# First x asked for after VectorE's first memset, and 16 warm-up matmuls

## The reference

```python
y = x[b] @ weight[adapter_ids[b]].T              # 256 x 1024
logits = y @ gate_w.T + expert_bias              # 4 experts
one_hot = one_hot(argmax(logits))
z = einsum('nh,erh->ner', y, lora_A)             # 4 experts x rank 8
delta = einsum('ner,ehr->neh', z, lora_B) picked by one_hot
out = x[b] + y @ W_up.T + delta
```

## Time and profile before

| what | us |
|---|---|
| median of three runs | 374.62 |
| the profiled execution | 374.81 |
| its span, first to last instruction | 373.0 |
| TensorE busy in it | 367.5 |
| VectorE, ScalarE busy | 262.4, 159.4 |
| first real matmul | 8.45 after the span's start |

### The profile page before, as it was taken

One profiled execution on the slowest core, in us unless ns is written; L12 is line 12 of the kernel. 1 busy time (PEld: TensorE's weight loads), 2 busy tenths in 40 slices (PEclk: granted clock), 3 DMA queues, 4 the chain that ended last, 5 costly groups with the idle time before them and its releaser, 6 DMA issues.

```text
span 373.0 us, 6260 instructions
## 1 busy us (share of the span) xinstructions
PE 367.5 (99%) x2348; PEld 334.7 (90%) x2348; DVE 262.4 (70%) x519; ACT 159.4 (43%) x320; POOL 6.6 (2%) x18
## 2 busy tenths in 40 slices
PE   7999999999999999999999999999999999999996
PEld 5888888888888999889998899989999899988996
DVE  4777587696758988678755786567874777746752
ACT  5667363642527543465115651155513553144300
POOL 1000500000000000000000000000000000000000
PEclk9999999999999999999999999999999999999999
DMA  7999975871069730687026760376404861160002
GB/s 244 402 394 312 408 286 182 325 226 57 0 192 340 252 119 0 226 302 243 21 96 210 270 216 3 147 250 231 163 2 178 324 213 76 49 234 0 2 1 114
DMA packets 19598, 68.19 MB, mean 183 GB/s; under 512 B 2288, under 2 KB 2416, under 8 KB 19568
## 3 DMA queue, kind: packets, MB, share of 16 engines
q1 hardware_dynamic: 19280, 66.74, 50.0%
q10 hardware_dynamic: 288, 1.05, 0.8%
HBM read 59.39 MB, written 8.39 MB: 182 GB/s over the span
## 4 chain that ended last, share of the span: by engine, by line
PE 97%; SPq 1%; DMA 1%; DVE 0%; issue 0%; ACT 0%; DVEq 0%
PE ps_y L785 31%; PE ps_u L796 19%; PE ps_y L787 16%; PE ps_v L796 10%; PE ps_p L796 5%; PE ps_u L803 2%; PE ps_v L803 2%; PE ps_u L807 2%; PE ps_v L805 2%; PE ps_u L805 2%; PE ps_v L807 2%; PE ps_p L816 1%; DMA w_raw<-w_dram 1%; SPq L241 1%; PE ps_p L847 0%; PE ps_v L847 0%
## 5 line engine op out<-in xcount | busy, mean ns | idle before, releaser
L785 PE MATMUL ps_y<-x_hilo,w_hi 128*128 128x512 f32 x512 | 178.3, 392 | 0.3 <-DVE w_lo L510 0.3
L787 PE MATMUL ps_y<-x_hilo,w_lo 128*128 128x256 f32 x512 | 143.2, 280 | 0.0
L785 PEld LDWEIGHTS ps_y<-x_hilo,w_hi 128*128 128x128 f32 x512 | 95.8, 187 | 22.1 <-DVE w_lo L510 0.8
L787 PEld LDWEIGHTS ps_y<-x_hilo,w_lo 128*128 128x128 f32 x512 | 96.7, 189 | 0.1
L517 DVE TENSOR_TENSOR w_lo<-w_raw,w_hi 128x512 fp32r<-128x512 f32 x126 | 81.3, 688 | 16.9 <-ACT w_hi L376 16.2
L376 ACT CAST w_hi<-w_raw 128x512 fp32r<-128x512 f32 x126 | 71.8, 624 | 3.4 <-DMA w_raw<-w_dram 3.3
L391 ACT COPY small<-ps_y 128x256 f32<-128x256 f32 x64 | 23.8, 372 | 107.2 <-PE ps_y L787 107.0
L562 DVE TENSOR_TENSOR y_raw<-ps_y,small 128x256 f32<-128x256 f32 x64 | 27.2, 425 | 47.1 <-ACT small L391 47.1
L796 PE MATMUL ps_u<-up_lo,y_parts 128*128 128x256 f32 x192 | 38.4, 281 | 0.0
L796 PE MATMUL ps_u<-wide_hi,y_parts 128*128 128x256 f32 x192 | 34.8, 293 | 0.0
L573 DVE TENSOR_TENSOR y_parts<-y_raw,y_parts 128x512 fp32r<-128x512 f32 x50 | 32.5, 687 | 1.3 <-ACT y_parts L394 0.9
(11 more groups left out here) (108 smaller groups left out, 393.7 us busy)
## 6 DMA issues: line engine op xcount, KB each, us to landing
w_raw<-w_dram SPq DMA_DIRECT2D x64, 512.0 KB, 4.4
rows<-x_dram SPq DMA_DIRECT2D x16, 512.0 KB, 5.7
out_dram<-rows SPq DMA_DIRECT2D x15, 512.0 KB, 2.6
x_raw<-xT_dram SPq DMA_DIRECT2D x14, 512.0 KB, 5.0
up_raw<-w_up_dram SPq DMA_DIRECT2D x8, 512.0 KB, 12.4
wide_stage<-w_up_dram SPq DMA_DIRECT2D x4, 512.0 KB, 14.0
thin_stage<-w_up_dram SPq DMA_DIRECT2D x4, 512.0 KB, 9.4
x_raw<-xT_dram ACTq DMA_DIRECT2D x2, 512.0 KB, 4.2
```

Source lines behind the costliest of these rows:

```text
L785: pe.matmul(ps_y[c % 2][:, :], w_hi[:, n % RING, cols], x_hilo[:, :, k, :], start=(k == 0), stop=False)
L787: last = pe.matmul(ps_y[c % 2][:, S:2 * S], w_lo[:, n % RAWS, cols], x_hilo[:, 0, k, :], start=False, stop=(k == KC - 1))
```

## The change

ScalarE waits, ahead of its two requests for the first x, for `warm_step` to be 1, that is for the end of VectorE's first memset. Nothing else in ScalarE's order moves. The number of matmuls on zeros goes from 18 to 16.

```diff
-    WARM = 18
+    WARM = 16
...
+            act.wait_ge(warm_step, 1)
             for d in range(XD):
                 ks = slice(d * XS, (d + 1) * XS)
                 act.dma_start(x_raw[:, 1, ks, :], xT[0, :, ks, :]).then_inc(x_raw_in[d], 16)
```

## The result

The changed kernel takes 375.67 us, the median of 15 runs (375.01 to 375.89); the kernel before takes 375.08 in 15 runs (374.54 to 375.44). The ratio is 1.0014, with a 95% interval of 1.0008 to 1.0021: slower by 0.5 us, clear of noise, and inside the 0.2% that was set as the bound of "same". The profiled execution took 375.59, with a span of 373.8, against 374.81 and 373.0 before.

A forecast was written before the change was run, and what follows sets the result against it. TensorE bounds the kernel, leaving only the start: x's second half landing late puts the first real matmul at 9.32, plus 5.69 makes 15.01 against 14.38, so +0.6 us on 374.62, median 375.2; range 374.1 to 375.8.

The forecast's parts named there:

- What bounds the kernel: Whole kernel: TensorE is busy throughout the middle, so only the start and the wait ahead of block 2 can move the end.
- the hole ahead of block 2: Batch 0, between blocks 1 and 2: TensorE waits 0.24 us for VectorE's y_full, behind slice 2; absorbs part of a shift.
- (1) The wait: ScalarE at the start: x asked for 0.71 us later, at about 1.45; the table load behind it costs nothing.
- (3) The index load: SyncE's second register load at the start: falls from 1.99 to 1.49 us, so w is asked for at 3.75, not 4.25.
- rival B: SyncE's start: index load falls to 0.46, w asked for at 2.72, first real matmul 9.65, +0.96, 375.6; chance 0.18.
- (4) The sharing: DMA engines at the start: x and w share, x's second half lands last at 7.50, first real matmul at 9.32.
- the halves: DMA engines at the start: x and w each get half of 414 GB/s; x through at 7.05, w's slice about 7.1.
- x undisturbed: DMA engines at the start: one bound of the sharing, x not slowed by w, its second half there at 6.46.
- the 1.82 behind x's half: Start: 1.82 us of casts and subtractions from the landing of x's second half to the first real matmul.
- (5) The warm-up: TensorE's start: two zeros matmuls fewer end the warm-up at 7.65 instead of 8.11, which gains nothing.
- The sum: Whole kernel: first real matmul at 9.32 plus 5.69 gives 15.01 instead of 14.38; about +0.6 us, median 375.2.
- Rival A: SyncE's start: index load stays 1.99, x's second half lands 6.88, first real matmul 8.70, 374.9; chance 0.18.

The follow-up runs named there:

- Both late: Changed kernel with SyncE held by dummy memsets so w is asked for at 4.14, x still after the memset: 375.18 against 374.90 before, ratio 1.0008.
- 16 matmuls alone: Kernel before with 16 warm-up matmuls instead of 18, no wait of ScalarE: 374.79 against 374.93, ratio 1.0004.
- before, slices 1 to 3 held: Kernel before, SyncE asking for slice 1 of w only once x's second half landed, 14 warm-up matmuls: 375.28 against 374.90, ratio 1.0013.
- slice 0 and x alone: Changed kernel, SyncE waiting for both halves of x to land before asking for slice 1 of w: 375.69 against 374.93 before, ratio 1.0021.
- the wait alone: Changed kernel with 18 warm-up matmuls instead of 16: 375.56 against 374.93 for the kernel before, ratio 1.0017.
- with the 2 KB request: Changed kernel, ScalarE asking for the 2 KB bias ahead of its wait instead of SyncE: 375.70 against 374.93 for the kernel before, ratio 1.0022.
- half of x at the start: Changed kernel, only x's second half waiting for the memset, the first asked for at 0.74: 375.28 against 374.82 before, ratio 1.0017.
- x's second half behind: Changed kernel, x's second half on SyncE's queue behind slice 0, its third quarter taken later, 14 warm-up matmuls: 376.75 against 374.82 before, ratio 1.0055.
- the same, first half at the start: x's second half on SyncE's queue behind slice 0, but without ScalarE's wait, first half asked for at 0.74: 376.31 against 374.82 before, ratio 1.0037.

## Why the prediction held, and where it didn't

It gave 375.2 from a median of 374.62, +0.6; measured is +0.6 between the medians of 15 (375.67 - 375.08), 0.5 by the ratio. The sign, the size and the place are right. But several of its steps were off and made up for each other: that the number came out so near is in part luck.

- **What bounds the kernel: right.** Nothing moved but the start, the hole ahead of block 2, and the cadence of batch 0.
- **(1) The wait: right.** x's requests went out at 1.44, 0.70 later, and the table load ran from 2.33, hidden.
- **(3) The index load: mis-sized.** I took 1.49 from the sums of later pairs, which hide that the second load of a pair alone took 0.45 to 0.46 in four of them and 1.44 to 1.52 in two. Here it is 0.46 to 0.47, once 0.69, when x's transfer isn't under way. That is the end I had named as rival B. The 459 ns amid full traffic misled me into thinking that traffic doesn't matter; at the start it does, in all six profiles in which x is asked for at 0.74.
- **(4) The sharing: it costs, as I had it, but the share and the loser were wrong.** By the halves x's second half should have landed last, at 7.50 (and at 7.83 with the load at 0.46); it was cast at 6.98. Slice 0 was to be cast at 7.7 and was at 8.27. Nothing was shared evenly: x, asked for first, had the engines alone until 5.60, and of the 1.24 MB moved by 6.50 only 0.19 are w's. In bytes my bound "x undisturbed" was the nearer one, though x's last packets then came until 6.8 beside w's, and by 6.2 where w was asked for late. The Trainium skill's rule that I had set beside mine ("DMA: Bandwidth & Descriptors", Queues, rings and completion order) doesn't show as an even split here, since SyncE's queue got no turn between its request at 2.90 and 5.60. Whether its packets waited at the engines or hadn't been made yet, no view tells. From 5.60 on, slice 0 also shared with slices 1 to 3 (below). So the 1.82 behind x's half never counted: 0.92 behind slice 0 did. Rival B's price was too high for this reason: 9.65 against 9.19.
- **(5) The warm-up: right, nothing** (1.0004, 0.9993 to 1.0014), with one thing that I had considered only for the changed kernel: in executions where the clock rises late, the 18 matmuls hold up the kernel *before* (8.87, where slice 0 allowed 8.48).
- **The sum.** It was +0.87 at the first matmul by me and is +0.74 measured. The hole ahead of block 2 was given back as said, since slices 1 and 2 were there in good time (ScalarE's casts of them ran from 10.02 without a wait). Then +0.28 of cadence that no step had.
- **Rival A as an experiment.** Both late gives the first matmul at 8.70, the very figure of A. That is luck again: A had x's second half land last, at 6.88, and in the run slice 0 did (x's third cast began by 6.5). The difference from there to 9.19 is the price of asking for w early, slices 1 to 3 included: 0.49, and 0.6 by the second profile of the changed kernel (9.33). The measured medians say the same less sharply, 1.0008 against 1.0014 with intervals that overlap.

What this price is made of can be read from the queues: what SyncE's queue had moved 0.6 us ahead of slice 0's cast, by when slice 0 (0.52 MB) should be through. The 0.6 is an estimate from the profiles.

| kernel | w asked for | its first packet | MB moved |
|---|---|---|---|
| before, two profiles | 4.25, 4.21 | 5.2 to 5.3 | 0.54, 0.54 |
| 16 matmuls alone | 4.09 | 5.1 to 5.2 | 0.54 |
| before, slices 1 to 3 held | 4.11 | 5.1 to 5.2 | 0.52 |
| both late | 4.14 | 5.6 to 5.7 | 0.55 |
| slice 0 and x alone | 2.71 | 5.6 to 5.7 | 0.52 |
| changed, two profiles | 2.90, 2.72 | 5.6 to 5.7 | 0.65, 0.75 |
| the wait alone | 2.71 | 5.6 to 5.7 | 0.72 |
| with the 2 KB request | 2.71 | 5.8 to 5.9 | 0.61 |
| half of x at the start | 4.31 | 5.3 to 5.4 | 0.64 |
| x's second half behind | 2.89 | 4.1 to 4.2 | 1.00 |
| the same, first half at the start | 3.98 | 5.0 to 5.1 | 0.54 |

In the changed kernel and its like, 0.09 to 0.23 MB of what was asked for behind slice 0 moved ahead of its end, where with w asked for late hardly anything did. At the 0.4 MB per us of these stretches that is 0.2 to 0.6 us, an estimate in which the 0.49 fits. The row with half of x at the start says that requests piling up early aren't the only way to it: w was asked for 1.0 ahead of its first packet there, and 0.12 MB passed all the same. In the last two rows SyncE's queue carries x's second half too.

So the change does what it says to the index load, and that is worth less than nothing: x 0.70 late costs 0.25 at the first matmul, w 1.2 us early costs another 0.5, and 0.24 of the sum is absorbed at block 2. None of the variants beat the kernel before; 16 matmuls alone can't be told from it. The split into 0.25 and 0.5 rests on single profiles, whose first matmul differs by 0.14 between two of the same kernel.

Open is by what order a DMA engine serves what is asked for in one queue: x's second half, directly behind slice 0, took 7.27 us where it took 4.6 in the kernel before. Open too is what picks the cadence: idle gaps of 0, 0.31, 1.26, 1.27, 1.63 and 1.69 us ahead of the first real matmul went with 2.83, and gaps of 0, 1.39, 1.53, 1.66 and 1.71 with 2.77. A hole changed it in the first profile of the kernel before, and didn't where slice 1 was held back.

## What to carry to other kernels

A request that goes out earlier isn't a transfer that lands earlier. Here w's first packet moved between 5.6 and 5.7 whether it was asked for at 2.90 or at 4.14, and slice 0 was used later for the earlier request. Count the bytes asked for ahead of the landing that the first matmul needs last, and those queued up behind it too, and read from each queue's own bytes who really moved. When an early start is bought by delaying another transfer, move one and hold the other, as in the run with both late: the delay of x had looked hidden and cost 0.25, and the earlier w had looked like a gain and cost 0.5.

## What the runs showed of the hardware

- A register load from DRAM took 0.46 to 0.47 us (once 0.69) with no large transfer under way and 1.72 to 2.05 with 0.5 or 1 MB asked for at 0.74, though later in the kernel 0.46 occurs beside full traffic.
- With 1 MB asked for at 1.44 on one queue, 512 KB asked for on another at 2.71 to 2.90 or at 4.14 had its first packet between 5.6 and 5.7 either way.
- TensorE's granted clock fell to half within a gap of 4.22 us between matmuls (1.00 to 0.50 at about 10.0), and not in gaps of up to 1.71 at the start.
- Sixteen warm-up matmuls took 5.3 to 6.5 us from one execution to another, since the moment at which their distance halves from 0.43 to 0.23 differs. The granted clock reads 1.00 in these stretches too, so the distances tell it and the clock's row doesn't.
- At full clock a pair of 512 and 256 columns takes 0.347 or 0.353 us (2.77 or 2.83 per block of 8 pairs), and from block 2 of batch 0 on each profile kept to one of the two to the batch's last block, stalls aside. Over eight blocks that is 0.4 us, as much as the changes that were measured here, so a single profile can't price a step of a few tenths.
